# A pool of eighteen buffers for the weight pieces, a piece-by-piece layout for the quantized weights, sums shared by two engines, and W_k loaded first

## What is computed

```python
def reference(x, w_qkv, w_o, w1, b1, w2, b2, gamma, beta):      # x: [8, 4096, 1024]
    x = x + layernorm(linear_attn(layernorm(x), w_qkv, w_o))
    x = x + layernorm(ffn(layernorm(x), ...))
def linear_attn(x, W_qkv, W_o):      # 16 heads of 64, chunks of 64 rows, k normalised by head
    y = S @ q + causal(q k^T) v;  S = S + v k^T          # state S carried from chunk to chunk
    return y @ W_o
def ffn(x, ...):
    h = layernorm(x) * gamma + beta
    h = gelu(qlinear(h, w1, b1));  return qlinear(h, w2, b2)
def qlinear(x, w, b):                # w1: [4096, 1024], w2: [1024, 4096]
    xq = round(x * 127 / max|x| per row)
    wq = clip(round(w / mean|w|), -1, 1)                 # the mean is over the whole matrix
    return (xq @ wq^T) * scales + b
```

## Time and profile before

| | |
|---|---|
| median of 3 runs | 1606.2 us (1605.7 to 1608.01) |
| the profiled execution | 1602.8 us |
| its span on the slowest core (core 2) | 1601.3 us |
| spans of the 8 cores | 1591.7 to 1601.3 us |
| busy share of PE, DVE, ACT, POOL | 91%, 70%, 41%, 18% |

### The profile page before, as it was taken

One profiled execution on the slowest core, in us unless ns is written; L12 is line 12 of the kernel. 1 busy time (PEld: TensorE's weight loads), 2 busy tenths in 40 slices (PEclk: granted clock), 3 DMA queues, 4 the chain that ended last, 5 costly groups with the idle time before them and its releaser, 6 DMA issues.

```text
span 1601.3 us, 26580 instructions; the slowest of 8 cores (1591.7 to 1601.3 us)
## 1 busy us (share of the span) xinstructions
PE 1459.8 (91%) x8948; PEld 723.0 (45%) x8948; DVE 1116.3 (70%) x1861; ACT 662.8 (41%) x1057; POOL 282.3 (18%) x211
## 2 busy tenths in 40 slices
PE   0488599999999998689999999999999999999997
PEld 0245355655555555334444444444444444444443
DVE  3755356677777876676777767777677776767764
ACT  1078477677555655333323232232322323223231
POOL 1111124555667775000000000000000000000000
PEclk9989899999999999999999999999999999999999
DMA  9968868988889786243342543424334243342422
GB/s 192 294 162 250 195 160 203 215 228 230 188 188 214 197 180 159 90 89 79 81 100 61 107 74 81 100 61 111 71 82 98 60 111 71 89 92 60 103 52 66
DMA packets 285045, 209.94 MB, mean 131 GB/s; under 512 B 246632, under 2 KB 248680, under 8 KB 284912
## 3 DMA queue, kind: packets, MB, share of 16 engines
q1 hardware_dynamic: 261776, 131.16, 36.7%
q0 software_dynamic: 23136, 77.08, 18.1%
HBM read 119.03 MB, written 33.55 MB: 95 GB/s over the span
## 4 chain that ended last, share of the span: by engine, by line
PE 66%; DMA 12%; issue 7%; ACT 4%; DVE 4%; DVEq 3%; POOL 2%; SPq 2%; ACTq 1%; POOLq 0%
PE pz L439 28%; PE pp L427 27%; DMA pc<-w 7%; PE pp L317 4%; DMA h1f<-h1t 3%; PE pp L335 2%; PE pp L403 2%; POOL lt L1102 2%; DMA kst<-w_qkv 1%; PE pp L418 1%; ACT pc L887 1%; SPq L1007 1%; DVEq L725 1%; DVEq L512 1%; DVE wqtp L569 1%
## 5 line engine op out<-in xcount | busy, mean ns | idle before, releaser
L427 PE MATMUL pp<-w1p,xq1f 128*128 128x512 fp8e4 x2048 | 457.0, 381 | 0.0
L439 PE MATMUL pz<-w2p,xq2f 128*128 128x512 fp8e4 x2048 | 447.1, 379 | 0.0
L439 PEld LDWEIGHTS pz<-w2p,xq2f 128*128 128x128 bf16 x2048 | 200.4, 98 | 241.6
L427 PEld LDWEIGHTS pp<-w1p,xq1f 128*128 128x128 bf16 x2048 | 195.8, 98 | 243.9 <-issue 19.9
L638 DVE TENSOR_REDUCE st<-gsb 128x1 f32<-128x1024 f32 x128 | 152.6, 1214 | 130.6 <-ACT gsb L895 130.4
L901 ACT ACT_TABLE_LOAD x31 | 39.8, 1283 | 469.5 <-DVE st L677 469.5
L1102 POOL TENSOR_SCALAR lt<-pc,st 128x1024 bf16<-128x1024 f32 x64 | 192.5, 3008 | 143.6 <-DMA pc<-w 83.2
L895 ACT ACTIVATE gsb<-pp,st 128x1024 f32<-128x1024 f32 x128 | 142.1, 1110 | 104.5 <-PE pp L427 98.7
L317 PE MATMUL pp<-wk,h1f 128*128 128x512 bf16 x512 | 121.2, 389 | 68.9 <-DMA h1f<-h1t 33.2
L317 PE MATMUL pp<-wv,h1f 128*128 128x512 bf16 x512 | 125.8, 390 | 15.7 <-ACT kt L838 12.6
L1123 POOL DMA_DIRECT2D pc<-w x128 | 82.8, 647 | 215.7 <-ACT pc L887 115.0
(11 more groups left out here) (114 smaller groups left out, 1511.5 us busy)
## 6 DMA issues: line engine op xcount, KB each, us to landing
pc<-w POOLq DMA_DIRECT2D x128, 512.0 KB, 5.9
xs<-x SPq DMA_DIRECT2D x32, 512.0 KB, 5.7
x1s<-xs SPq DMA_DIRECT2D x32, 512.0 KB, 4.6
xs<-x1s SPq DMA_DIRECT2D x32, 512.0 KB, 3.6
out<-xs SPq DMA_DIRECT2D x32, 512.0 KB, 3.1
wost<-w_o POOLq DMA_DIRECT2D x8, 512.0 KB, 49.3
kst<-w_qkv SPq DMA_DIRECT2D x8, 512.0 KB, 19.5
wv<-w_qkv POOLq DMA_DIRECT2D x1, 2048.0 KB, 31.6
```

Source lines behind the costliest of these rows:

```text
L427: mi = PE.matmul(half(n, h), lhsT=xf[:, kk, :], rhs=w1q[:, kk % 4, c0:c0 + 512, kk // 4], start=False, stop=(kk == 7), skip_group_check=True)
L439: mi = PE.matmul(PZ[:, h * 512:(h + 1) * 512], lhsT=xq2f[:, t % 2, kk, :], rhs=w2q[:, kk % 16, h * 512:(h + 1) * 512, kk // 16], start=(kk ...
```

## The change

W_q becomes one tile `wq`, loaded by one DMA. SP issues the chunks of W_k straight behind the first two tiles, then the two turning DMAs, then the bias; POOL holds back W_q, W_v and W_o until chunk 5 of W_k has landed. `h1t` becomes two buffers (the second one in the room of a second `kf`, which becomes single). The quantized weights lie piece by piece: a piece is one block of 4x128 in `w1p[:, j]` or `w2p[:, c, 4b:4b+4]`, so that the moving operand of a 128x512 matmul is now four blocks of 128 instead of one row of 512. All 18 buffers (two of `pc`, eight of `pc1`, eight of `pc2`) form one pool, dealt out when the program is built: a buffer of `pc1` or `pc2` can be used until the quantized piece that covers it is written. A load is issued as soon as the one that held its buffer has been consumed two places back in the order. Seven pieces of w1 and five of w2 (`hold`) are summed last and stay where they are until they are quantized, so that 116 loads are left of 128. Of the 64 sums 27 go to DVE (`piece_vsum`): the twelve held ones and fifteen of the first ones. w2 is quantized in natural order, the last quantizations are dealt to iteration 30 instead of 29, and PE waits for w2's turned pieces only ahead of `ffn2(0)`. `gam` and `bet` lie in the room of `wq` and now wait for the last `q_half`.

```diff
-    wqa = at("wqa", O_WQA, [8, 512], BF16)
-    wqb = at("wqb", O_WQB, [8, 512], BF16)
+    wq = at("wq", O_WQA, [8, 1024], BF16)
-    w1p = at("w1p", O_W1, [4, HID], BF16)
+    w1p = at("w1p", O_W1, [NWP, 4, 128], BF16)
-    w2p = at("w2p", O_W2, [16, D], BF16)
+    w2p = at("w2p", O_W2, [8, 16, 128], BF16)
-    h1t = at("h1t", O_H1T, [1024], BF16)
+    h1t = [at("h1t0", O_H1T, [1024], BF16), at("h1t1", O_KF + 2048, [1024], BF16)]
-    kf = at("kf", O_KF, [2, 8, 128], BF16)
+    kf = at("kf", O_KF, [8, 128], BF16)
...
-    gap = 12
-    line = [("sum", 0, j) for j in range(NWP)] + [("sum", 1, j) for j in range(gap)]
+    gap, hold = 12, (7, 5)
+    order = [list(range(hold[k], NWP)) + list(range(hold[k])) for k in range(2)]
+    line = [("sum", 0, j) for j in order[0]] + [("sum", 1, j) for j in order[1][:gap]]
...
-    cost = {"sum": 1.0, "quant": 1.75}
-    share = sum(cost[p[0]] for p in line) / (T - 2)
+    cost = {"sum": 1.0, "quant": 1.6}
+    first, last = 0, T - 2
+    share = sum(cost[p[0]] for p in line) / (last - first + 1)
...
+    def on_dve(p):
+        return p[0] == "sum" and (p[2] < hold[p[1]]
+                                  or place[p] < NWP + gap and place[p] % 5 in (1, 3))
...
+    held = [-1] * 10 + [8] * 8
+    count = [0] * 18
+    loads, where, prior = [], {}, {}
+    for p in pieces:
+        if p[0] == "quant" and p[2] < hold[p[1]]:
+            where[p] = where[("sum", p[1], p[2])]
+            continue
+        stays = p[0] == "sum" and p[2] < hold[p[1]]
+        end = place[("quant", p[1], p[2])] if stays else place[p]
+        own = range(2 + 8 * p[1], 10 + 8 * p[1]) if stays else range(18)
+        z = min((b for b in own if end < covered[b]), key=lambda b: held[b])
+        count[z] += 1
+        where[p] = (z, 16 * count[z])
+        prior[p] = (held[z], count[z] > 1)
+        held[z] = end
+        loads.append(p)
...
                         mi = PE.matmul(half(n, h), lhsT=xf[:, kk, :],
-                                       rhs=w1q[:, kk % 4, c0:c0 + 512, kk // 4],
+                                       rhs=w1q[:, c0 // 128:c0 // 128 + 4, kk % 4, :, kk // 4],
...
                 for k in range(4):
-                    PE.wait_ge(s_wtp[k], 16 * 2 * NWP // 4)
+                    PE.wait_ge(s_wtp[k], 16 * NWP // 4)
...
+        def piece_vsum(p):
+            buf, s_ld, landed = piece_buf(p)
+            V.wait_ge(s_ld, landed)
+            V.tensor_reduce(out=c1((acc1, acc2)[p[1]], p[2]), in_=buf, axis=AX.X, op=ALU.add,
+                            apply_absolute_value=True).then_inc(s_vabs, 1)
...
         def h1(t):
             A.wait_ge(s_r1, t + 1)
             if t >= 2:
-                A.wait_ge(s_h1tp[(t - 1) % 2], 16 * ((t - 1) // 2 + 1))
+                A.wait_ge(s_h1tp[t % 2], 16 * (t // 2))
...
-        GP.dma_start(out=wqa, in_=wsrc[:, :, 0:512]).then_inc(s_qld[0], 16)
+        GP.wait_ge(s_kld[5], 16)
+        GP.dma_start(out=wq, in_=wsrc[:, :, 0:1024]).then_inc(s_qld, 16)
...
+        def load(n):
+            p = loads[n]
+            buf, s_ld, _ = piece_buf(p)
+            if n >= 4:
+                GP.wait_ge(piece_buf(loads[n - 4])[1], piece_buf(loads[n - 4])[2])
+            o, used = prior[p]
+            if not used and where[p][0] >= 10:
+                GP.wait_ge(s_oc, 8)
+            if used and pieces[o][0] == "quant":
+                GP.wait_ge(s_q, nqua[o] + 1)
...
+            GP.dma_start(out=buf, in_=piece_src(p)).then_inc(s_ld, 16)
+
         GP.wait_ge(s_kc, 8)
+        n = 0
         for q, p in enumerate(pieces):
...
+            while n < len(loads) and prior[loads[n]][0] <= q - 2:
+                load(n)
+                n += 1
+            if p[0] == "quant":
+                below(p)
-        GP.wait_ge(s_Q, 2 * (T - 1))
+        GP.wait_ge(s_Q, 2 * T)
         GP.dma_start(out=gam[:], in_=gamma_h.partition_broadcast(128)).then_inc(s_gbl[0], 16)
```

More of the change, by code:

```diff
@@ L236, in build @@
                                             sem("ln5_r"), sem("zn"), sem("out_ready"))
-    gap = 12
-    line = [("sum", 0, j) for j in range(NWP)] + [("sum", 1, j) for j in range(gap)]
+    gap, hold = 12, (7, 5)
+    order = [list(range(hold[k], NWP)) + list(range(hold[k])) for k in range(2)]
+    line = [("sum", 0, j) for j in order[0]] + [("sum", 1, j) for j in order[1][:gap]]
     for j in range(NWP - gap):
-        line += [("sum", 1, gap + j), ("quant", 0, j)]
+        line += [("sum", 1, order[1][gap + j]), ("quant", 0, j)]
     line += [("quant", 0, j) for j in range(NWP - gap, NWP)]
-    line += [("quant", 1, 4 * c + b) for b in range(4) for c in range(8)]
-    cost = {"sum": 1.0, "quant": 1.75}
-    share = sum(cost[p[0]] for p in line) / (T - 2)
+    line += [("quant", 1, j) for j in range(NWP)]
+    cost = {"sum": 1.0, "quant": 1.6}
+    first, last = 0, T - 2
+    share = sum(cost[p[0]] for p in line) / (last - first + 1)
     plan = [[] for _ in range(T)]
-    spent, i = 0.0, 0
+    spent, i = 0.0, first
     for p in line:
-        while i < T - 3 and spent >= share * (i + (1.0 if i % 2 else 0.8)):
+        while i < last and spent >= share * (i - first + (1.0 if i % 2 else 0.8)):
             i += 1
@@ new lines, in build @@
+    nsum = [sum(1 for p in pieces[:q] if p[0] == "sum" and not on_dve(p))
+            for q in range(len(pieces) + 1)]
+    nvsum = [sum(1 for p in pieces[:q] if on_dve(p)) for q in range(len(pieces) + 1)]
+    nqua = [sum(1 for p in pieces[:q] if p[0] == "quant") for q in range(len(pieces) + 1)]
+    bufs = ([pc[:, k] for k in range(2)] + [pc1[:, k] for k in range(8)]
+            + [pc2[:, k] for k in range(8)])
+    covered = ([4 * NWP] * 2 + [place[("quant", 0, 4 * k)] for k in range(8)]
+               + [place[("quant", 1, 4 * k)] for k in range(8)])
@@ L288, in q_of, with piece_buf, sums_under @@
+    def piece_buf(p):
+        return bufs[where[p][0]], s_pl[where[p][0]], where[p][1]
+    def sums_under(k, z):
+        under = [place[p] for p in pieces
+                 if p[0] == "sum" and not on_dve(p) and where[p][0] == 2 + 8 * k + z // 4]
+        return nsum[max(under)] + 1 if under else 0
     def q_of(t, j):
@@ L495, in pe_program @@
                 ffn1(t + 1, [2, 3])
+            if t == 0:
+                for k in range(4):
+                    PE.wait_ge(s_wtp[k], 16 * 2 * NWP // 4)
             ffn2(t)
@@ L574, in quant_piece, with take_piece @@
                                    saturate=False).then_inc(s_q, 1)
+        def take_piece(p):
+            if p[0] == "sum":
+                piece_vsum(p)
+            else:
+                quant_piece(p)
         def w_total(k):
-            V.wait_ge(s_abs, NWP * (k + 1))
+            V.wait_ge(s_abs, nsum[max(place[("sum", k, j)] for j in range(NWP)) + 1])
+            V.drain()
             V.tensor_reduce(out=c1(tot, k), in_=(acc1, acc2)[k], axis=AX.X,
@@ L743, in dve_program @@
                     w_total(k)
-            now = [p for p in plan[t] if p[0] == "quant"] if 0 <= t < T else []
+            now = [p for p in plan[t] if p[0] == "quant" or on_dve(p)] if 0 <= t < T else []
             if two:
@@ L937, in act_program @@
                 gelu(0, 1)
-            now = [p for p in plan[t] if p[0] == "sum"] if t >= 0 else []
+            now = [p for p in plan[t] if p[0] == "sum" and not on_dve(p)] if t >= 0 else []
             for p in now[:1]:
@@ L995, in sp_program @@
             SP.dma_start(out=xs[:, t], in_=rows(x_h, t)).then_inc(s_xld[t], 16)
+        for kk in range(8):
+            SP.dma_start(out=kst[:, kk],
+                         in_=wqkv_h[kk * 128:(kk + 1) * 128, 1024:2048]).then_inc(s_kld[kk], 16)
+        for t in range(2):
+            h1_tp(t)
         SP.wait_ge(s_cst, 1)
```

123 lines of the change are left out of this document (40 added, 83 removed).

## The result

The changed kernel takes 1625.9 us in the median, against 1607.1 us for the kernel before, measured beside it. The ratio of the times is 1.0122, with a 95% interval of 1.0102 to 1.0142: 1.2% slower, where 2% faster was forecast. (On a few executions a whole die runs at a lower clock; all times and ratios from here on leave those out.)

What follows compares the result with a forecast made beforehand. PE was taken to bound the kernel, at its pace from 693 us, with holes before. 81 + 113 + 387.6 + 50.9 + 938.5 = 1571 us of span, 30 less than 1601.3; 1606.2 - 30 = 1576 us, range 1555 to 1601.

Steps and rivals of the forecast that it cites:

- A, -13: Start to out_proj(0): W_o's first chunk lands at 49 us, DVE's 17.5 us follow; out_proj(0) at 81, 13 us sooner.
- B, -18: Six iterations from out_proj(0) to out_proj(6): 15 us lost instead of 32.8, so 18 us less.
- I leave 4 us for each burst: Iterations 1 to 6: each of POOL's two bursts of about eight piece loads costs 4 us.
- The upper bound of 27 lost: Iterations 1 to 6: 27 us lost if both load bursts cost what was lost in the one.
- The step on the shared sums: Iterations 1 to 6: 17 sums put 21 us on DVE, which has 72 us free; ACT loses as much work.
- C, -19: 23 iterations from out_proj(6) to out_proj(29): fewer, earlier loads, 19 us less.
- I leave 12 of 31.5 us: Iterations 7 to 29: 12 us still lost, 1.4 for the threshold, 3 for last pieces, the rest DVE and ACT.
- most of POOL's 83 us goes: Iterations 7 to 29: most of POOL's 83 us wait for landing pieces goes, with twelve fewer loads and others issued earlier.
- D, +20: out_proj(29) to the second part's first matmul: four serial loads and comparisons, 8.85 us each; 50.9 instead of 30.9 us.
- E, 0: The second part, 938.5 us: matmuls with a moving operand of four blocks of 128 take no longer.
- The transfers fight: Rival, iterations 7 to 29: piece loads make turning DMAs land 9 us later, about 1675, mostly 1600 to 1620; 12%.
- Looking ahead gives C nothing: Rival, iterations 1 to 29: DVE's and ACT's own order made the holes, most stay, 1598 us; 11%.

Runs made afterwards that it cites:

- experiment 11: The changed kernel with W_o's eight chunks ahead of W_v in POOL's first loads: ratio 1.0122 to the kernel before.
- experiments 3 and 4: 3: the kernel before, eight loads first filling its second buffer set wait for sums, 0.9949; 4: the paced kernel with one row buffer's wait, 0.9954.
- experiment 5: The paced kernel with the 15 early sums back on ACT, DVE keeping only the 12 held pieces: ratio 1.0025.
- the paced kernel: The changed kernel, each piece load before the first comparison also waiting for the sum of the piece eight loads before: ratio 0.9976.
- experiment 8: The paced kernel, on POOL comparisons ahead of loads not due soon, and those loads only when due within eight places (the cap): ratio 0.9889.
- 15: The paced kernel plus cap, comparisons ahead, two loads in flight, h1's turning first, W_o before W_v, last loads and gam, bet earlier: 0.9745, 1563.4 us.
- experiments 1 and 2: 1: the paced kernel, ratio 0.9976; 2: the changed kernel with two piece loads in flight in place of four throughout, ratio 1.0021.

## Why the prediction was wrong

**A, -13: mis-sized.** Rate, order and DVE's 17.5 us were right, the first landing of W_o was not: 55.8 us, not 49, and outside the 45 to 54 given for it. The last chunk landed at 24.3 + 42.9 = 67.2 us, and the eight within 11.4. The step had this near: the same bytes, so no last landing much before 65.5, and 13.2 us earlier is 52.3. Taking 49 instead, for one DMA of W_q, is the term that failed. The step also left out that W_v can end A: experiment 11.

**B, -18: the step that failed is "I leave 4 us for each burst".** The two bursts were foreseen, and that iterations 3 and 5 would be the longer ones, but they cost 15 to 20 us each. (They were placed in iterations 1 and 3; on core 6 they begin at 107.75 us, in iteration 2, and at 157.37, as iteration 4 begins.) The price was taken low because the stall of the earlier trace rows was read as that of a row buffer made worse by a burst; experiments 3 and 4 showed it to be the burst alone, and the row buffer to be worth nothing once loads are paced. Read so, would have given the right price: 18 us for one. The upper bound of 27 lost, "if both bursts cost what was lost in the one", isn't the sum it names: two times 18, with the 4 and the 3 left for other things, is 43, and 40 were lost (138.1 against 98.0). The step on the shared sums was right that DVE has the room; what ACT gains is 7 us of B (experiment 5). Without bursts B is 102.8, better than the 113 forecast.

**C, -19: the step that failed is "I leave 12 of 31.5 us".** The premise, "most of POOL's 83 us goes", came true, and its gain came where it was sought: in iterations 16 to 29 the losses fell from 17.4 to 8.1 us (medians of the cores). But 5 to 7 of what is left there are iteration 18, with w2's threshold, for which the step had 1.4; and iterations 7 to 15, where the quantizations begin, lost 16.6 instead of 9.1, for which the step had no term. Waits from 230 to 638 us (in total, times, longest), POOL's as in the earlier trace rows and then PE's for h1's turnings:

```profile
POOL pc L1151 <- DVE wqtp L592: 99.9, 25, 12.4
...
POOL pc L1151 <- DVE st L584: 11.1, 1, 11.1
...
POOL lt L1132 <- DMA pc<-w: 2.2, 2, 1.5
...
PE pp L350 <- DMA h1f<-h1t: 17.6, 5, 8.4
```

For landing pieces POOL waits 2.2 us now. It waits 99.9 ahead of loads for DVE's quantizations, 36.2 of them in iterations 19 to 29, which lose 2.3 us in all, and 11.1 at the load ahead of the first comparison, behind which the turning of iteration 9 stands. On the eight cores PE waits 10 to 18 us in C for h1's turnings, before at most 3.5. The prediction asked how early loads are issued, and not what stands behind a load that must wait for its buffer. With the comparisons ahead and the cap C fell from the 409.9 of the paced kernel to 395.8 (experiment 8); in 15, with two loads in flight and the other edits as well, to 382.2, below the forecast 387.6. What of this each edit is worth alone stays open, and so does iteration 18.

**D, +20: right.** +19.0; a load and its comparison took 7.9 us in the mean (637.85 to 669.62, four times), not 8.85, the rest as drawn. **E, 0: right.**

**The rivals.** "The transfers fight" is nearest to what came, with 12%. Its mechanism, turnings landing 9 us later, was too mild (13.5 later in bursts), and its place was the first fills of the pool, not all of C. The Trainium skill's rule cited there ("DMA: Bandwidth & Descriptors", Queues, rings and completion order: an engine takes packets from the queues in turn) agrees in its direction with experiments 1 and 2: with fewer loads queued beside them, turnings land in 6.5 and 5.8 us instead of 18.7. Experiment 2, which changes only how many loads are under way at a time, shows that this number matters here, and not only that loads are queued at all. "Looking ahead gives C nothing" has the right number for C, but not its reason: looking ahead took 9 us from iterations 16 to 29, and iterations 7 to 15 gave most of them back.

## What to carry to other kernels

More buffers give a queue more to do at once, not only earlier: when a pool is filled for the first time, or many of its buffers come free behind one wait, say what paces the issues, and look which small, urgent transfer shares the engines in that time. On an engine that works in order, a load that waits for its buffer is a wait of everything behind it, so what is due now goes ahead of what is due in fifteen places. And a stall in the trace of before may have its cause in the neighbour that the change makes larger: here one added wait in the kernel before would have told the burst from the buffer.
